# Linear attention and FFN on one core: attention in steps of 64 tokens as float32 products in 32x64 and 64x32 tiles, the masked states written by GpSimd

## The reference

```python
q, k = phi(proj(Wq, bq)), phi(proj(Wk, bk))      # phi(x) = elu(x) + 1
v = proj(Wv, bv)
def step(carry, inp):                            # one chunk of 128 tokens of one head
    S, z = carry
    scores = where(tril, einsum('bqd,bkd->bqk', qi, ki), 0)
    num = einsum('bqk,bkd->bqd', scores, vi) + einsum('bqd,bde->bqe', qi, S)
    kcum = cumsum(ki, axis=1) + z
    den = sum(qi * kcum, axis=-1)
    return (S + einsum('bkd,bke->bde', ki, vi), z + ki.sum(axis=1)), num / den
x = x + attention(layernorm(x)) @ Wo.T + bo
x = x + x' + 0.5 * (silu(h @ w1 + b1) @ w2 + b2)  # x' = layernorm(x), h = its layer norm, scaled
```

## Time and profile before

| | us |
|---|---|
| median of three runs | 1517.6 |
| the profiled execution, its span | 1513.5 |
| TensorE busy | 1490.1 |
| VectorE, ScalarE, GpSimd busy | 1283.0, 1129.9, 680.4 |
| one step from the middle of the loop | 45.63 |

### The profile page before, as it was taken

One profiled execution on the slowest core, in us unless ns is written; L12 is line 12 of the kernel. 1 busy time (PEld: TensorE's weight loads), 2 busy tenths in 40 slices (PEclk: granted clock), 3 DMA queues, 4 the chain that ended last, 5 costly groups with the idle time before them and its releaser, 6 DMA issues.

```text
span 1513.5 us, 40860 instructions
## 1 busy us (share of the span) xinstructions
PE 1490.1 (98%) x14936; PEld 1309.0 (86%) x14936; DVE 1283.0 (85%) x2587; ACT 1129.9 (75%) x1917; POOL 680.4 (45%) x469
## 2 busy tenths in 40 slices
PE   8799999999999999999999999999999999999998
PEld 7588889888888888888888888888888888888887
DVE  6888888888888888888888888888888888888875
ACT  3487777887777887777887777887777877777863
POOL 3244344544344544345444445444445443445444
PEclk9899999999999999999999999999999999999999
DMA  7856775556765556765557765557755557755460
GB/s 198 200 121 145 180 163 141 130 134 152 180 142 157 124 135 162 180 151 138 131 128 173 180 134 152 129 125 180 180 132 145 132 131 180 180 128 138 111 139 29
DMA packets 153945, 222.98 MB, mean 147 GB/s; under 512 B 20032, under 2 KB 71488, under 8 KB 153920
## 3 DMA queue, kind: packets, MB, share of 16 engines
q1 hardware_dynamic: 152560, 222.63, 60.9%
q10 hardware_dynamic: 1360, 0.01, 0.1%
HBM read 138.69 MB, written 83.89 MB: 147 GB/s over the span
## 4 chain that ended last, share of the span: by engine, by line
PE 94%; DVE 2%; DMA 1%; POOL 1%; issue 1%; ACT 0%; SPq 0%; POOLq 0%; DVEq 0%
PE ring L343 35%; PE num L538 8%; PE ring L426 8%; PE sc L496 7%; PE ring L427 7%; PE sc L343 6%; PE num L505 4%; PE num L343 3%; PE state_acc L343 3%; PE ring L373 3%; PE state_acc L496 2%; PE ring L572 2%; PE state_acc L519 2%; PE num L427 1%; PE num L426 1%; PE num L555 1%
## 5 line engine op out<-in xcount | busy, mean ns | idle before, releaser
L1147 POOL TENSOR_TENSOR s_lo<-silu_f,s_hi 128x512 fp32r<-128x512 f32 x256 | 343.7, 1348 | 534.8 <-ACT s_hi L997 534.7
L343 PE MATMUL ring<-w_hi,s_hi 128*128 128x256 f32 x992 | 280.9, 283 | 0.0
L343 PE MATMUL ring<-w_hi,s_lo 128*128 128x256 f32 x992 | 277.6, 280 | 0.0
L343 PE MATMUL ring<-w_lo,s_hi 128*128 128x256 f32 x992 | 277.5, 280 | 0.0
L682 DVE TENSOR_TENSOR probs<-sc,causal 128x512 f32<-128x512 f32 x320 | 208.1, 684 | 15.1 <-PE sc L496 7.1
L343 PEld LDWEIGHTS ring<-w_hi,s_hi 128*128 128x128 f32 x992 | 186.5, 188 | 12.2 <-DVE phi_q L728 12.0
L1042 ACT ACTIVATE x_hat<-x,hn_add,ln_rstd 128x256 f32<-128x256 f32 x128 | 66.6, 591 | 173.8 <-DVE hn_add L870 173.8
L986 ACT ACTIVATE silu_f<-ring,bias,scale 128x512 f32<-128x512 f32 x217 | 167.6, 772 | 32.8 <-PE ring L427 26.8
L426 PE MATMUL ring<-gt_hi,w_q 128*128 128x512 f32 x441 | 190.5, 432 | 0.0
L343 PEld LDWEIGHTS ring<-w_lo,s_hi 128*128 128x128 f32 x992 | 186.5, 188 | 0.0
L343 PEld LDWEIGHTS ring<-w_hi,s_lo 128*128 128x128 f32 x992 | 186.5, 188 | 0.0
(11 more groups left out here) (204 smaller groups left out, 3953.5 us busy)
## 6 DMA issues: line engine op xcount, KB each, us to landing
k_stack<-k_rows SPq DMA_DIRECT2D x192, 256.0 KB, 4.1
q_stack<-q_rows SPq DMA_DIRECT2D x384, 128.0 KB, 6.1
k_rows<-silu_f SPq DMA_DIRECT2D x128, 256.0 KB, 3.2
q_rows<-probs SPq DMA_DIRECT2D x128, 256.0 KB, 2.5
x_in<-in_x SPq DMA_DIRECT2D x32, 512.0 KB, 8.3
xb<-in_x SPq DMA_DIRECT2D x32, 512.0 KB, 7.9
out<-clip SPq DMA_DIRECT2D x64, 256.0 KB, 7.4
silu_f<-in_q SPq DMA_DIRECT2D x2, 512.0 KB, 9.0
```

The lines of the kernel that those rows point to most:

```text
L343: last = e.matmul(target, a, b, start=(n == 0), stop=(n == 3 * len(pairs) - 1))
L1147: sl.done(e.tensor_tensor(s_lo[:, j, :], silu_f[:, j % SLOTS, :], s_hi[:, j, :].bitcast(F32), ALU.subtract))
```

## The change

Attention goes in steps of 64 tokens (two halves r of each chunk, now called m), all in plain float32: the stacks, their splits and their DMAs are gone. Scores of a half are 32 products in 32x64 tiles, a pair of heads' 32 rows of phi_k against q_mask (phi_q with every other head zeroed, written by ScalarE). VectorE masks four times a step. The sums k·v of each 64 tokens are made apart (`chunk_states`, one call for each r, the second waits for the first), VectorE adds them up with a scan into kv_sums, and GpSimd writes from it the seven masked states of each half of the features, one instruction each (`snapshots`), after ffn_lo(3) and before ffn_lo(4) in its order. The masked scores times v are products in 64x32 tiles, those with the states in 128x32 tiles. `hold` adds 1 to a counter that nobody waits for. The denominators of batch i+1 are summed at the end of step i, VectorE takes the reciprocals at once (256 elements), and SyncE copies them to all the features' rows in 16 DMAs (32 KB each). The values of batch i+1 are projected in step i. PSUM banks are handed out anew, clip, state, hn2, rb and out_t have tiles of their own, and ScalarE's silu and rounding are no longer one behind the other.

The diff, cut to its core:

```diff
+            def scores(t):
+                w.need(phi, 0, 2 * t)
+                w.need(q_par, 0, t)
+                free_bank(w, f"sc{t}", present)
+                for m in range(C):
+                    for g in range(PAIRS):
+                        rows = slice(PW * g, PW * (g + 1))
+                        for r in range(2):
+                            last = e.matmul(sc[HALF * r:HALF * (r + 1), g, m * P:(m + 1) * P].rearrange("p (a q) -> p a q", a=2),
+                                            phi_k[rows, t, chunk(r, m)], q_mask[rows, t, :, chunk(r, m)],
+                                            start=True, stop=True, skip_group_check=True)
+            def chunk_states(r):
+                w.need(kt_sb, 0)
+                w.need(v_sb, 0)
+                if r == 0:
+                    free_bank(w, "kv", present)
+                else:
+                    w.need(half_pe, 0)
+                w.hold()
+                toks = slice(HALF * r, HALF * (r + 1))
+                for t in range(T):
+                    for m in range(C):
+                        for g in range(PAIRS):
+                            last = e.matmul(kv_bank[PW * g:PW * (g + 1), t, :, 2 * m + r],
+                                            k_tok[toks, m, t * P + PW * g:t * P + PW * (g + 1)],
+                                            v_pad[toks, m, t * PAIRS + g, 0:4:3, :],
+                                            start=True, stop=True, skip_group_check=True)
+            def values(t):
+                if t == 0:
+                    free_bank(w, "num", present)
+                w.need(masked, 0, 2 * t + 1)
+                w.need(v_sb, 0)
+                w.hold()
+                for m in range(C):
+                    for odd in range(2):
+                        for r in range(2):
+                            toks = slice(HALF * r, HALF * (r + 1))
+                            for g in range(PAIRS):
+                                last = e.matmul(num[PW * g:PW * (g + 1), r, num_of(r, t, m)],
+                                                v_pad[toks, m, t * PAIRS + g, 2 * odd:2 * odd + 2, :],
+                                                probs[toks, t, g, m, odd, :],
+                                                start=(t == 0 and m == 0 and odd == 0), stop=(odd == 1), skip_group_check=True)
+            def from_states(t):
+                w.need(snap, 0, t)
+                for c in range(1, 2 * C):
+                    m, r = divmod(c, 2)
+                    for g in range(PAIRS):
+                        last = e.matmul(num[PW * g:PW * (g + 1), r, num_of(r, t, m)],
+                                        state[:, t, c - 1, PW * g:PW * (g + 1)], phi_q[:, t, chunk(r, m)],
+                                        start=False, stop=False, skip_group_check=True)
...
+            ffn_in(0)
+            ffn_in(1)
             k_transposes(0)
             k_transposes(1)
+            scores(0)
             fc1(0)
+            x_transposes(0)
+            x_transposes(1)
             fc1(1)
+            fc1(2)
+            chunk_states(0)
             scores(1)
+            chunk_states(1)
+            fc1(3)
+            fc1(4)
             values(0)
+            fc1(5)
             values(1)
+            from_states(0)
+            from_states(1)
             fc1(6)
             fc1(7)
             if N:
+                project_kq()
+                project_v(0)
+                project_v(1)
             output_projection()
+            if Fn:
+                fc2(0)
+                fc2(1)
             if N:
+                denominators()
+            if Fn:
+                fc2(2)
+                if N:
+                    fc2(3)
...
+            def mask(t, h):
+                w.need(sc_pe, 0, t)
+                w.need(av_pe, -1, t)
+                masked.done(e.tensor_tensor(
+                    probs[:, t, 2 * h:2 * h + 2, :, :, :].rearrange("p g m a q -> p (g m a) q"),
+                    sc[:, 2 * h:2 * h + 2, :].rearrange("p g (x q) -> p (g x) q", q=HALF),
+                    causal[:, None, :].to_broadcast([P, 4 * C, HALF]), ALU.mult))
+            def sum_states():
+                w.need(upd_pe, 0)
+                kv_sb.done(e.tensor_tensor_scan(kv_sums[:, :], scan_keep[:, :], use_bank("kv"), 0.0, ALU.mult, ALU.add))
...
             ffn_sum(2)
+            mask(1, 0)
+            mask(1, 1)
+            sum_states()
+            ffn_sum(3)
+            ffn_sum(4)
+            ffn_sum(5)
+            attention(0)
+            attention(1)
+            ffn_sum(6)
+            ffn_sum(7)
...
+            ffn_scaled(3)
+            ffn_scaled(4)
+            ffn_hi(2)
+            ffn_silu(3)
+            ffn_scaled(5)
+            ffn_hi(3)
+            ffn_silu(4)
...
+        kv_view = kv_sums[:, :].rearrange("p (t x c) -> p t c x", t=T, c=2 * C)
+            def snapshots(t):
+                w.need(kv_sb, 0)
+                w.need(num_pe, -1)
+                shape = [P, STATES, PAIRS, PW]
+                snap.done(e.tensor_tensor(
+                    state[:, t, :, :].rearrange("p n (g x) -> p n g x", x=PW),
+                    kv_view[:, t, 0:STATES, :][:, :, None, :].to_broadcast(shape),
+                    head_ones[:, :].rearrange("p (g x) -> p g x", x=PW)[:, None, :, :].to_broadcast(shape), ALU.mult))
+            for j in range(4):
                 ffn_lo(j)
+            snapshots(0)
+            snapshots(1)
+            if A:
+                w.need(x_again, 0)
+                e_xb.done(e.tensor_tensor(xb[:, :, :], xb[:, :, :], bias_o[:, None, :].to_broadcast([P, C, D]), ALU.add))
+            ffn_lo(4)
+            ffn_lo(5)
...
+            def sp_reciprocals():
+                w.need(rden, 1)
+                w.need(at_l, 0)
+                for t in range(T):
+                    for half in range(2):
+                        g = 2 * t + half
+                        for a in range(DUP):
+                            e.dma_start(rb[a:P:DUP, t, 2 * P * half:2 * P * (half + 1)], den_rows[32 * g:32 * g + 32, :])\
+                                .then_inc(rb_in.sem, 16)
```

More of the change, by code:

```diff
@@ new lines, in build, with ffn_bank, z_bank, use_bank @@
+        NEXT_USES = {"xt0", "xt1", "k0", "q0", "k1", "q1", "v0", "v1", "den"}
+        TAIL = ((1, 0), (6, 3), (4, 2))
+        def ffn_bank(j, t, A):
+            return bank(BANKS[f"f{j}{'ab'[t]}"][0]) if A else bank(TAIL[j % 3][t])
+        def z_bank(n):
+            return bank(BANKS[f"z{n}"][0])
+        def use_bank(use):
+            return bank(BANKS[use][0])
+        def qk_bank(is_q, m):
+            return use_bank("kq"[is_q] + str(m))
+        def chunk(r, m):
+            return slice(m * P + r * HALF, m * P + (r + 1) * HALF)
@@ L345, in pe_split3 @@
             return last
-        def pe_projection(e, w, n, m, s, present):
-            if m:
-                w.need(masked["kq".index(n)], s - 1)
-            else:
-                free_bank(w, n + "0", present)
-            cols = slice(m * P, (m + 1) * P)
-            last = pe_split3(e, qk_bank("kq".index(n), m)[:, :], [
-                ((w_hi[n][:, t, cols], w_lo[n][:, t, cols]), (xt_hi[:, t, :], xt_lo[:, t, :])) for t in range(T)], lambda t: w.need(xt_l, s, t))
-            qk_pe.done(last)
         def pe_tokens(e, w, n, lhs, use, present, event):
@@ L435, in fc2 @@
                     free_bank(w, f"z{n}", present)
-                def slices(j):
-                    w.need(sh, shift, j if not N else FT - 1)
-                    w.need(sl, shift, j if not N else FT - 1)
+                w.need(sh, shift)
+                w.need(sl, shift)
                 toks = slice(c * P, (c + 1) * P)
-                last = pe_split3(e, ring_bank(f"z{n}")[:, h * D:(h + 1) * D], [
-                    ((s_hi[:, j, toks], s_lo[:, j, toks]), (w2_hi[:, j, :], w2_lo[:, j, :])) for j in range(FT)], slices)
+                last = pe_split3(e, z_bank(n)[:, h * D:(h + 1) * D], [
+                    ((s_hi[:, j, toks], s_lo[:, j, toks]), (w2_hi[:, j, :], w2_lo[:, j, :])) for j in range(FT)])
                 if h:
@@ L526, in values @@
-            def values(u):
-                t, c = divmod(u, C)
-                for r in range(2):
-                    w.need(masked[r], 0, u)
-                w.need(v_sb, 0, c)
-                if c == 0 and Fn:
-                    w.need(f_b, -1, 0)
-                if u == C:
-                    w.need(rden, 0)
-                for odd in range(2):
-                    for pair in range(HT // 2):
-                        last = e.matmul(
-                            num[t][32 * pair:32 * pair + 32, c * P:(c + 1) * P],
-                            v_pad[:, c, t * HT // 2 + pair, 2 * odd:2 * odd + 2, :],
-                            masked_scores(u)[:, 2 * pair + odd, :],
-                            start=(c == 0 and odd == 0), stop=(odd == 1), skip_group_check=True)
-                av_pe.done(last)
```

1043 lines of the change are left out of this document (413 added, 630 removed), and 6 rows, old and new, of the table BANKS.

## The result

The changed kernel took 1705.96 us in the median of 4 runs (1701.54 to 1706.87) where the kernel before took 1518.28 (4 runs): a ratio of 1.1235, 95% interval 1.1211 to 1.1258. Slower, as forecast, but by 188 us and not by 53, and outside the range, which ended at 1645. The profiled execution spans 1704.8 us.

The account below looks back on a forecast made before the run. TensorE's issue was taken as the bound before, at 45.63 us a step. After, 47.46 us a step, 1.83 more over 31 steps (+57), and -4 outside them: 1517.6 + 53 = 1570 us, range 1512 to 1645.

Parts of the forecast that it names:

- the path: Chain of one step through scores, masks, s_lo of slice 3, two GpSimd snapshots and state products: 42.46 + 2s = 47.46 us.
- the clock's fall: TensorE's clock dropping in the new gap before the state products: not in the sum, 1.7 us for one fall as rival.
- the rates of TensorE's small tiles: Attention products on TensorE, eight tiles at a time as taken: 7.7 us a step for 12.6, TensorE alone 40.7.
- what lies outside the steps: First batch loses 48 filler products and the copies it waited for, its long wait stays in part: -4 us.
- The snapshot's price: Each GpSimd snapshot of 896 elements, s in the sum: 2.5 us taken, ends 2.11 and 2.85.
- Rival 1: Snapshots' strided read on GpSimd slow throughout, 2.85 us each or more: 48.2 us a step, 1593 us; chance 0.18.
- rival 2: TensorE's clock falls in the new gap, 1.7 us a fall, more if in each step: 1596 to 1623 us; chance 0.15.
- Rival 3: TensorE's row tiles don't run side by side, 4.5 us a step more work: up to 1667 us; chance 0.10.
- scores at 0.11 for 16 instructions: Sign to look for in the changed profile: TensorE's score products take 0.11 us per 16 instructions.
- Rival 4: Faster: snapshots under 1.67 us each, path shorter than TensorE's saving; 1496 us at 1.3 us each; chance 0.14.
- VectorE at 33 to 35 us, ScalarE at 33, GpSimd at 26: Work per step of the other engines: VectorE about 33 us, 35 at most, ScalarE about 33, GpSimd about 26.
- copy of reciprocals: SyncE's 16 copies, 7.4 us of issue and up to 6.1 to land, costed at nothing behind 13 us of cover.

Follow-up runs that it names:

- pool_first: The changed kernel with both snapshots on GpSimd two places further ahead in its queue, behind the second low half instead of the fourth: 1496.03 us, ratio 0.9838.
- contig: The changed kernel with the snapshots reading the sums in memory order instead of every eighth element, so the output differs: 1662.52 us in one run.
- same_size: The changed kernel with fill_wide's added products, less 12 instructions of the last state's products so the loop's code does not grow: 1634.43 us, ratio 1.0776.
- sums_first: pool_first with VectorE's order changed: upper mask of the second scores, then state sums, then lower mask, bank waits fitted: 1471.34 us, ratio 0.9665.
- fill: The changed kernel with 12 and 6 products of the 128x128 identity ahead of the first and second state products: 1805.21 us, ratio 1.1878.
- fill_wide: The changed kernel with 3 and 1 identity products of 512 columns ahead of the state products, 8 instructions more per step: 1800.02 us, ratio 1.1813.
- code_8: sums_first with 8 one-instruction products of 256 columns ahead of the state products for each half of the features, 16 a step: 1751.97 us in one run.
- dve_snap: The changed kernel with both snapshots on VectorE, behind the fifth feed-forward sum, instead of GpSimd: 1535.01 us, ratio 1.0106.
- dve_contig: dve_snap with the sums read in memory order as in contig, so the states hold other sums: 1480.13 us in one run.

## Why the prediction was wrong, by its own steps

Three terms failed, and not the path: the clock's fall, put at nothing in the sum and at 1.7 us as a rival; the rates of TensorE's small tiles; and what lies outside the steps, put at -4. The sum was off by 136 us (1706 for 1570). By steps of 47.46 forecast and 51.21 measured, 31 of them make 116; the rest lies outside them.

- **The path was right.** Scores, masks, s_lo of slice 3, snapshots, state products: the chain went through them, the s_lo before the snapshots took 1.28 us, and pool_first shows by a move in the queue alone that this wait (with what it draws along) was the whole loss.
- **The snapshot's price was right**: 2.52 us measured, 2.5 taken, between 2.11 and 2.85. Rival 1 did not come. The Trainium skill's GPSIMD Engine Reference, Performance pitfalls for Q7 kernels, adds half for such a stride; the runs contig and after show 2.08 to 2.52, a fifth.
- **The clock: rival 2, given a chance of 0.15, was the case, in every step.** The argument against it (one idle microsecond at 12 to 13 us left the level alone) was weak beside the earlier trace rows, which showed a fall after 3.4 us at 0.23 us busy; the gap here has 0.25 us busy in 3.6. The price was low as well: 1.7 us a fall was half of 3.4 us, but the level stays down for some 6.9, and the earlier trace rows had already shown it down for 10.2 us, from 68.03 to 78.27. same_size against the kernel after: 2.44 us a step, 76 us in 31 steps, over half of the error (the two runs differ by 72 us in all).
- **TensorE's tiles: the term was too small.** Rival 3 (they don't run side by side) did not hold, since four at a time would be 14.4 ns for the values, but the rates are lower than eight full tiles give. From start to start the values took 10.0 ns for the 7.2 forecast (1.84 us for 256 instructions), the scores 14.9 for 13.6, the sums k·v 8.9 for 7.5. TensorE's work was forecast at 40.7 us a step; sums_first shows about 42.8. These three rates make 1.1 of the 2.1 us; where the rest lies was not worked out. The prediction's sign "scores at 0.11 for 16 instructions" did not fit its own sum, which gives 0.22; 0.24 was measured. On the path of the kernel after, by its timeline, the state products of the second half came 0.95 us late, most of it from these groups; with the clock held in same_size the step is 48.77, 1.31 over the forecast, 41 us in all. What the other 0.36 is, was not tried.
- **Outside the steps: -4 forecast.** Span less 31 medians is 117.3 us after and 99.0 before: +18. The stalls put down to issue grew by 17.8 us (19.4 from 1.6), nearly all in the first batch, the first pass of the loop and the last steps, where code runs for the first time; the runs fill, fill_wide and code_8 show what TensorE does when it has to load code. A second cause stands beside it, and no run separates the two: the clock was lower there. The first 100 us, before and after (columns as above, the clock third from the end):

```profile
0.00:100.00 100.00, 82.75 (x774) 70.86 (x774) 78.58 (x155) 52.30 (x90) 30.86 (x34) 0.93 0.75 182
```
```profile
0.00:100.00 100.00, 68.54 (x1167) 59.49 (x1168) 59.01 (x114) 40.75 (x70) 25.15 (x34) 0.79 0.31 88
```

- **Code to load.** That 1717 matmul and load records in a step (859 and 858) in place of 929 also have to be loaded stood nowhere in the prediction.
- **Rival 4** (faster, if a snapshot costs under 1.67 us; 1.65 by its own sum) was right that a short path makes the kernel faster, and wrong that only the duration can shorten it: pool_first is faster at 2.61 us a snapshot, by its place in the queue.
- **VectorE at 33 to 35 us, ScalarE at 33, GpSimd at 26** were right (35.15, 32.58, 26.11), and no copy of reciprocals was waited for. The other scan, of phi_k (1.96 us in the median for 1.31), grew too, but was hidden.

So 136 is 76 for the clock, 41 for the tiles and what comes with them, 22 for the edges, and -3 because the forecast started from a median 4.1 us above its profiled span, where the kernel after has 1.2. The chances treated the rivals as exclusive; the range had no room for a fall in every step together with slower tiles.

## What to carry to other kernels

When an instruction moves to a free engine, ask where it stands in that engine's queue before asking what it costs: 5 us of snapshots behind two remainders for which nobody was waiting yet cost 12%, and the same instructions two places further ahead made the kernel 1.6% faster, 3.3% with the sums moved up as well. The 3.3 us for which TensorE waited here were paid twice, once as idle time and once as the clock that fell behind them (2.44 us a step); the 1.65 us of dve_snap were paid once. And count instructions as well as columns: this loop lay within 8 matmul instructions, with their weight loads, of a cliff of 6 to 7.5 us per pass, which the row of the instruction queue (27 packets, or 280) tells at a glance. Last, look at single instructions behind a median: 1.09 us in dve_contig stood for pairs of 2.04 and 1.08.

## What the runs showed of the hardware that had not been expected

- **TensorE's code loading.** With 8 matmul instructions more in the loop the instruction queue moved 280 packets (4.59 MB, 16.4 KB each) for 27, 8 or 9 more in each pass, and a step grew by 5.9 us (fill_wide against same_size) or, with 16 more, about 7.5 us (code_8 against sums_first, less the work added where TensorE was not idle). Both hold what the clock loses behind the stalls. The Trainium skill, Runtime: NRT & Kernel Launch, Instruction fetch mechanics, gives TensorE 2048 instructions in blocks of 256 and calls the cost of crossing a block mostly hidden. A limit of that kind would fit the jump, though no run counted the waits and other instructions that share it; that crossing is mostly hidden does not agree with stalls of 1.89 and 0.70 us in the midst of a step of code_8.
- **The rate of small tiles**, from start to start: 14.9 ns in 32x64 tiles of 128 columns, 10.0 in 64x32 of 64 (both the same in either order of the tiles), 8.9 in 64x32 of 32. What sets it, issue, weight loads or something else, was not tried.
- **A stride of eight floats in one operand** costs GpSimd 0.44 us for 896 elements (contig) and VectorE 0.7 us (first batch of dve_snap and dve_contig). A VectorE snapshot that begins while GpSimd is at work takes 0.95 us more, strided or not.
- **The falls of the clock keep step with the loop**: in the kernel after, from 259 to 1539 us, they came 51.2 us apart, once in each step, each 6.8 us long; in contig, at 49.83, falls of 3.4 and of 6.8 us took turns, and the steps went from 48.5 to 50.7.
